# Two-layer decoder on one core: the four value products of the memory attention become one part of TensorE's order, and the orders of four engines are searched anew

## The reference, cut to what matters

```python
x = _layernorm(x + _L0_attn_ref(x, ...))        # station A, windowed
x = _layernorm(x + _L0_xattn_ref(x, ctx, ...))  # station B, cross
x = _layernorm(x + _L0_ffn_ref(x, ...))         # station X, experts
x = _layernorm(x + _L1_attn_ref(x, ...))        # station C, decayed
x = _layernorm(x + _L1_xattn_ref(x, ctx, ...))  # station E, memory
x = _layernorm(x + _L1_ffn_ref(x, ...))         # station F, feed forward
```

## Time and profile before

| | before |
|---|---|
| median of 3 runs | 1128.7 us (1123.98 to 1131.87) |
| profiled execution: its own time | 1128.63 us |
| profiled execution: span of the trace | 1126.8 us |
| PE busy | 989.2 us, 88% of the span |
| DVE busy | 943.9 us, 84% |
| ACT busy | 751.5 us, 67% |
| POOL busy | 145.0 us, 13% |
| mean granted clock of TensorE | 0.959 |

### The profile page before, as it was taken

The page is one execution under the profiler, slowest core; times in us unless marked ns, Lnnn a source line. Parts: engine busy times, 40 slices in busy tenths (PEclk is TensorE's granted clock), DMA queues, the critical chain, the costliest instruction groups (busy, mean ns, idle before and its releaser), DMA issues.

```text
span 1126.8 us, 19792 instructions
## 1 busy us (share of the span) xinstructions
PE 989.2 (88%) x7038; PEld 699.1 (62%) x7038; DVE 943.9 (84%) x2541; ACT 751.5 (67%) x1854; POOL 145.0 (13%) x401
## 2 busy tenths in 40 slices
PE   4877789999999999999999999999999998898642
PEld 2654556676757676767677676757676666565321
DVE  3977666689898989899999989898989896857854
ACT  2233454758686868778686768686877777667653
POOL 2001110101111020202020111111020201010000
PEclk8879999999999999999999999999999999999875
DMA  6922113020211202020303020111202000000000
GB/s 210 332 84 71 31 57 94 1 66 20 66 38 40 64 29 74 20 85 10 94 10 94 1 83 21 57 47 38 65 29 65 11 11 19 1 20 1 10 9 10
DMA packets 36626, 58.90 MB, mean 52 GB/s; under 512 B 6784, under 2 KB 15872, under 8 KB 36016
## 3 DMA queue, kind: packets, MB, share of 16 engines
q1 hardware_dynamic: 36528, 57.64, 16.5%
HBM read 28.65 MB, written 4.19 MB: 29 GB/s over the span
## 4 chain that ended last, share of the span: by engine, by line
DVE 50%; PE 31%; ACT 12%; issue 4%; POOL 2%; DMA 0%; SPq 0%; ACTq 0%; DVEq 0%; POOLq 0%
PE bank_c L443 8%; DVE area_f L1247 8%; PE bank_e L443 6%; PE bank_a L443 5%; DVE area_a L987 5%; DVE neg_top L1180 4%; DVE area_a L1031 4%; ACT squares_out L1321 3%; DVE area_f L1238 3%; PE bank_f L443 3%; DVE x L875 2%; DVE area_f L1256 2%; DVE area_a L1035 2%; PE bank_x L443 2%; DVE area_f L1262 2%
## 5 line engine op out<-in xcount | busy, mean ns | idle before, releaser
L1247 DVE SCALAR_TENSOR_TENSOR area_f<-area_f,w_convw 128x254 f32<-128x254 f32 x256 | 111.9, 479 | 9.2 <-ACT area_f L1542 6.9
L1309 ACT ACTIVATE area_bx<-bank_x 128x512 f32<-128x512 f32 (+1 forms) x144 | 70.1, 498 | 37.9 <-PE bank_x L637 21.5
L1180 DVE TENSOR_REDUCE neg_top<-bank_e 128x4 f32<-128x512 f32 x128 | 80.5, 682 | 11.2 <-PE bank_e L443 10.5
L1542 ACT ACTIVATE area_f<-area_f,w_convb,w_convw 128x256 f32<-128x256 f32 x128 | 70.0, 596 | 27.1 <-DVE area_f L1238 26.8
L987 DVE TENSOR_TENSOR area_a<-area_a 128x512 f32<-128x512 f32 x112 | 73.3, 683 | 11.0 <-ACT area_a L1309 10.0
L1031 DVE TENSOR_TENSOR area_a<-area_a 128x512 f32<-128x512 f32 x112 | 74.5, 684 | 0.9 <-DMA area_a<-area_a 0.6
L1309 ACT ACTIVATE area_a<-bank_a 128x512 f32<-128x512 f32 (+1 forms) x80 | 44.0, 550 | 42.1 <-PE bank_a L443 31.1
L1309 ACT ACTIVATE area_bx<-bank_c 128x512 f32<-128x512 f32 x64 | 34.5, 539 | 53.9 <-PE bank_c L443 51.1
L1513 ACT ACTIVATE area_e<-bank_e 128x512 f32<-128x512 f32 x128 | 68.4, 594 | 1.4 <-PE bank_e L797 1.4
L1035 DVE TENSOR_TENSOR area_a<-area_a 128x512 f32<-128x512 f32 x96 | 65.8, 685 | 0.2
L443 PE MATMUL bank_e<-area_e,chosen_v 128*32 128x512 f32 x256 | 56.9, 604 | 5.1 <-ACT area_e L1513 4.6
(11 more groups left out here) (313 smaller groups left out, 2670.0 us busy)
## 6 DMA issues: line engine op xcount, KB each, us to landing
area_a<-area_a SPq DMA_DIRECT2D x96, 224.0 KB
area_a<-in_xT SPq DMA_DIRECT2D x16, 256.0 KB, 2.9
x<-in_x SPq DMA_DIRECT2D x16, 256.0 KB, 2.9
area_bx<-in_ctxT SPq DMA_DIRECT2D x16, 256.0 KB, 2.6
area_d<-in_ctxT SPq DMA_DIRECT2D x16, 256.0 KB, 2.7
y<-x SPq DMA_DIRECT2D x16, 256.0 KB, 2.2
w_wqkv_e<-in_wqkv_e SPq DMA_DIRECT2D x1, 3072.0 KB, 12.5
area_f<-in_raw SPq DMA_DIRECT2D x2, 1024.0 KB, 11.8
```

The lines of the kernel that those rows point to most:

```text
L1180: dve.tensor_reduce(top[:, b, :, r, 0].rearrange("p (par c) -> p c par", c=DC), bank_e[r][:, :].rearrange("p (c par k) -> p c par k", c=DC ...
L1247: last = dve.scalar_tensor_tensor(c4[:, i, :, dst], h4[:, i, :, src], cwt3[:, 2 * jj + i, k:k + 1], c4[:, i, :, dst], ALU.mult, ALU.add)
L1309: return act.activation(dst, src, ACT.Copy)
L1542: last = act.activation(c4[:, i], h4[:, i], ACT.Identity, bias=w["convb"][:, j:j + 1], scale=cwt3[:, j, 1:2])
```

## The change

On PE the four value products of a sequence become one part: one wait for the fourth exponential, four products, one mark on `e_pv`. Station E has 11 parts a group on PE and no longer 17. ACT's waits on `e_pv` are counted anew: the first exponential of the second sequence waits for the one mark of the first sequence, the other three wait for no product, and the copy to `turned_e` waits for one mark. The arithmetic, the tiles and the DMAs are the same.

The strings of SP, PE, DVE and ACT are others; POOL's is the same. Of what moved, apart from the joined parts:

- PE, groups 1 to 11: the joined products of the second sequence stand where its last three stood before; the single one, which stood between X.10 and C.4 or next to it, is gone. In group 13 the joined products of the second sequence stand behind X15.9, not ahead of it.
- From group 5 on, up to the emptying stage, the orders of PE, DVE and ACT hold only a few short moves; no division (L1197, L1201) changes its place among DVE's large parts.
- Between groups 3 and 4, DVE takes F3.0 ahead of C4.4, and PE takes X6.1 and F3.0 ahead of C4.12 and E4.0 (`FXCACEBFXFAE` becomes `FXCAXFCEB`).
- SP, groups 6 to 15: A.2 is ahead of B.0 of the same turn, not behind it.

```diff
 ORDER = {
     "SP": (
-        "SASABCSASASASSBSSAAABAAABAAACAABACBAACFABAACFABAACFABAACFABAACFABAACFABAACFABAACFABAACFABAACFABACFCFCFFF"
+        "ASSBCASASASSBASSSAAABAAABAAACAAABCBAACFAABACFAABACFAABACFAABACFAABACFAABACFAABACFAABACFAABACFAABCFFCFCFF"
         "F"
     ),
     "PE": (
...
-        "ACAXFCEEEEXCEXCXEXCECFXCEEEXECFECEACACFXCACEBFXFAEBFXABXFBXAEXFBEBAXCAFCEEEEXCEXCXEXCECXFCEEEXECFECEACAX"
...
+        "XCEXECFECEACACFXCAXFCEBFAEBFXABXBFXAEXBFEBAXCFACEXCEXCXEXCCXFCEXECFECEACAXCFCACEBFXFAEBFXABXFBXAEXFBEBAX"
...
     "DVE": (
...
-        "AAAFAFFFECXAFCFEEEEXAEEAFEEAXFAEXFBAFFAAFFBXBFAFFFFXAECFFAAFCACAXAFAAAAEAAAFAFFFECXAFCFEEEEXAEEAFXEEFAAB"
...
+        "AAFAFAFFEXCAFCFEEEEXAEEAFEEAXFAEFXBAFFAAFFBXBFAFFFFXAECFFAAFCACAXAFAAAAEAAAFAFFFEXCAFFCEEEEXAEEFAXEEFAAB"
...
@@ memory(g) on PE
                     yield
+                    pe.wait_ge(e_exp, 8 * g + 4 * b + 4)
                     for r in range(4):
-                        pe.wait_ge(e_exp, 8 * g + 4 * b + r + 1)
-                        mm(bank_e[0][group[r], :], [(mv[:, b, :], pT_e[:, r * 4 * P:(r + 1) * 4 * P])]).then_inc(e_pv, 1)
-                        yield
+                        last = mm(bank_e[0][group[r], :], [(mv[:, b, :], pT_e[:, r * 4 * P:(r + 1) * 4 * P])])
+                    last.then_inc(e_pv, 1)
+                    yield
                     pe.wait_ge(e_pv_out, 2 * g + b + 1)
@@ memory(g) on ACT
                         act.wait_ge(e_logits, 8 * g + 4 * b + r + 1)
-                        if b:
-                            act.wait_ge(e_pv, 8 * g + r + 1)
+                        if b and r == 0:
+                            act.wait_ge(e_pv, 2 * g + 1)
...
-                    act.wait_ge(e_pv, 8 * g + 4 * b + 4)
+                    act.wait_ge(e_pv, 2 * g + b + 1)
                     copy(turned_e, bank_e[0][:, :]).then_inc(e_pv_out, 1)
```

More of the change, by code:

```diff
@@ L79 @@
-        "EEEFEEEEEEEFEFEFFFFFFFFFF"
+        "AAAASAASSBSSBAAASABABAAABBSBXBXAAXAXAXBASXABSXAXABBXXXXXABAXBAXBABXAXAXBXABXCAXCXCXCXXCXCAXCAXCACCACXCAC"
+        "XEBXEBABEBXBEBACXAECXECECXXECXCXCXEAXECECACXACCFCAEBFBEFXABFXBXAEXFBEBACFAXCEXCEXCXEXCCFXCEFXECECEACACFX"
+        "CACXEBFAEFBFXABXFBXAEXFBEBACXAFCEXCEXCXEXCCFXCEXECFECEACACFXCACXEBFAFEBFABXFXBXAEXFBEBACXAFCEXCEXCXEXCCF"
+        "XCEXECFECEACACFXCAXFCEBFAEBFXABXBFXAEXBFEBAXCFACEXCEXCXEXCCXFCEXECFECEACAXCFCACEBFXFAEBFXABXFBXAEXFBEBAX"
@@ new lines @@
+        "CFACEXCEXCXEXCCXFCEXECFECEACAXCFCACXEBFAFEBFXBAXBFXAEXFBEBAXCFACEXCEXCXEXCCXFCEXECFECEACAXCFCACXEBFAFEBF"
+        "XBAFXBXAEXFBEBAXCFACEXCEXCXEXCCXFCEXECFECEACAXCFCACXEBFAFEBFXBAXBFXAEXFBEBAXCFACEXCEXCXEXCCXFCEXECFECEAC"
+        "AXCFCACXEBFAFEBXFBAFXBXAEXFBEBAXCAFCEXCEXCXEXCCXFCEXECFCEAECAXCFCACXEBFAFEBFXBAFXBXAEXFBEBAXCAFCEXCEXCXE"
+        "XCCXFCEXECFECEACAXCFCACXEBFAFEBFBXAFXBXAEXFBEBAXCFACEXCXECXEXCCXFCEXECFECEACAXCFCCXEBFEBFBFXBXFXEXFEBFBX"
+        "CECXECEXCXFXECXCXCXEFECECFCXCCFCEFCFCECFXCEXEFXFXECEXCXEXCFXEXCFXEXECECFCCCECFCEFCFEFCEFECECECFECECCEFEC"
@@ L91 @@
[L91 to L92 removed]
+        "SAAASAAAASSSSAAAAAAAAAAAAAAASASAAAAABAABASABAAAAAAAAAAAAAXAXSXSAAAAASXAABAXABAAAAAXAAAAAAAABXAXAAAXXAABA"
+        "BAXBAXAAAAAAAXAACAAAAACXCAXCXACAAAXAEEEEEEEEEAABBXBAAXEAAAAACXAAAAAACCAAXEEACFCXEEEEAAAAAEEFEXEFEFXBFFAA"
+        "BFFXBFAFFFFXAECFFAAFACCAFXAAAAAAEAFAFAFFEXCAFCFEEEEXEEAAFEEXAFEAFXBAFFAAFFBXBFAFFFFXAECFFAAFACCAXAFAAAAE"
@@ L93 @@
+        "EEEXAEEAFXEEFAAEBAFFAAFXFXBFBFAFFFFXAECFFAAAFCCAXFAAAAAEAAAFAFFXFECAFCFEEEEXAEEAFEEXAFXAEFABFFAABFFXBFFA"
+        "FFFXAEFCAFAFCACXAFAAAAAEAAFAAFFFXECAFCFEEEEXEEEFXEEFBFXFBFFXFFBFFFFXEFFXFCFCCXEFFFFEFCFCXEEEEFFEEEEEFXFC"
+        "FFFFXFFFXFEXFFCCFXFFFFFEXECFCFEEEEEEEEEFFCFFFCFEFCFFFFFFFEFCFEFCFFFEEEEFFEEEEEFFFFFFFFEFFFFFFFEFFFFFEFFF"
         "FFFFFFFFFFFFFFFFFFFF"
@@ L106 @@
-        "FCEFFFXEFFFXEEEFFXCECFXFXEFXCEEEXCCXEFXCFFFEXCXECEFCFCFCFCFEFEEEFECFEFCFFCEEEECCFEFCFFCFECEFCFFFEFFFFFEF"
-        "FFEEEEFFEFFFFEEEFEFEEFFFFEEFFFFFFFFFFFFFFFFFFFFFF"
+        "AASASSASASBSSBAAAASABABABABBBXBXAAAAXAXBAXXABABXXXXXSABXBBXAXBAAXBAAXBXBXAXBCAXBCXCXXCXCXCAXXCCACXACACAA"
+        "CXBXBBEBXBEEEEABCXAEBCXCEEEEXCXCXEXCCXCEACXXECEAXCAAFCABFBFABXFFXBFEFXBFFEEEEACFXFACBFEXCFXBXCEFCEXEECXE"
+        "CCCEFCFFFAEXECAXFXCAFAXBFAFBFABXFXFBEFFXBFEEFEEACXFAFCBEFXCFXBXCEFCEXEECXECCCEFCFFFAEXECAXFXCAFAXBFAFBFA"
@@ new lines @@
+        "BXFFXBFEXFBFEFEEEACXFAFCBEFXCFXXBCEFCEXEECXECCCECFFFFAEXECAXFXAFCAFXBFABFABXFXBFEFXFBFEEFEEACXFAFCBEFXCB"
+        "XFXCEXCFEEEXCECCCECFFFAFEXECAXFXCAFABFXFABFABXFXFFBEXFBFFEEEECAXFFACEBFXCFXBXCEFCXEEECXECCCECFFFAFXECAXE"
+        "XFCAAFXBFAFBFBAXFXFBEFXFBFFEEEEACXFFCBAEFXCFXBXCECXFEEECXECCCECFFFAFXECAXEXFCAAFXBFFABFBAXFXFBEFFXBFFEEE"
+        "ACXEFFCABEFXCFXBXCEXCFEEEXCECCCECFFFAFXECAXEXFCAAFXBFFABFBAXFXFBEFXFBFFEEEAECXFAFCEBFXCFXBXCEXCFEEECXECC"
+        "CECFFFAFEXCAEXXFCAAFXBFFABFABXFXFBEFXFBFFEEEAECXFAFCBEFXCFXBXCEFCXEEEXCECCCCEAFFFFXEXACXEFACAFXBFFABFBAX"
@@ L108 @@
+        "FXBFEFXFBFEEFEAXCFEAFCBEFXCFXBXCEFCXEEECXECCCECFFFAFEXCAEXXFCAAFXBFFABFBAXFXFBEFXFBFFEEEEAXCFFACBFEXBCXF"
+        "XCEFCXEEEXCECCCEFCFFAFXECAXEXACFXFBFBFBFXFXBFEFXFFEBEFEEXFCFEBCFXFBCFEXEXEECXECXCXCCEFCFFFXCEXEFCXFCFFCF"
+        "CFCEFFXEFFXFEEFEFXCECFXFXEFXCEEEXCCEXCFXFFFEXCXECEFCFCFCFCFEFEEEFECFFECFFCEEEECCFEFCFFCFECEFCFFFEFFFFFEF"
+        "FFEEEFEFFEFFEEEEFFEFEFFFFEEFFFFFFFFFFFFFFFFFFFFFF"
     ),
```

32 lines of the change are left out of this document (4 added, 28 removed).

## The result

The changed kernel takes 1132.44 us (median of 22 runs, 1130.25 to 1136.73) against 1130.28 us (22 runs) of the kernel before beside it: a ratio of 1.0026, 95% interval 1.0017 to 1.0036. A second comparison on another chip gave 1.0041 (1.0024 to 1.0058). So it is slower, by 2 to 5 us. The forecast was 1127.4 us, with no difference that can be measured as the likeliest; 1132.4 lies in the range (1116 to 1134) and within 1% of the kernel before, but the kernel moved the other way than forecast. A profiled execution of the changed kernel took 1134.5 us, with a span of 1132.7 us.

A forecast was written before the change was run, and what follows sets the result against it. The prediction took DVE's long piece and PE's short piece of each even-stage turn as the bound. Terms -1.96 - 0.54 + 1.25 = -1.25 us against 1128.63 us gave 1127.4 us, range 1116 to 1134.

The forecast's parts named there:

- What bounds the kernel: Even stage: DVE's work in the long piece or PE's in the short one sets the turn, despite PE's 96% busy.
- The half case: Rival: groups 1 to 11 gain some 0.5 us each as PE's lead helps ACT and DVE; 1121 us, chance 0.14.
- the case of PE as the bound: Rival: all 14 freed value product slots count, 13.7 us; 1116.2 us, chance 0.11.
- the late keys: Groups 3 to 4, keys' copy behind DVE's scaling: +1.25 us net, at most +1.74; as slower rival 1130.4 to 1133.4, chance 0.09.
- The split: An even-stage turn loops through two pieces: DVE fills 591.9 to 641.4 us, PE fills 581.3 to 591.9 us.
- the short piece: Part of a turn from 581.3 to 591.9 us, from the transposes of `att_e`; PE busy 10.56 of 10.60 us.
- The slots on the path: Single value products on the chain, groups 9 and 13: 0.98 us saved each; group 11: DVE's wait of 0.54 us goes.
- The other moves: Reordered parts, mostly in the filling and emptying stages: bounded at 3 us either way, taken as 0.
- The wait for the fourth exponential: Joined products wait for nothing in group 6 and end at the same time in group 15's emptying stage: cost 0.
- The clock rival: Rival: PE's longer wait before the even stage's transposes drops its clock; up to 95 us more, 1222 us, chance 0.03.

The follow-up runs named there:

- joined_alone: Kernel before, its order kept, with the four value products joined behind one wait for the fourth exponential: 1130.41 us, ratio 0.9998.
- spend_slot: Changed kernel, groups 1 to 11: memory attention's second division one station A product sooner on DVE, weights' copy directly behind the exponential on ACT: 1138.92 us, ratio 1.0069.
- turn4_full: Changed kernel with the turn from group 3 to 4 back in the order of before on every engine: 1131.35 us, ratio 1.0022.
- joined_four: Kernel before, its order kept, with the four value products joined, each waiting for its own exponential: 1126.56 us, ratio 0.9969; again 1126.51 us, 0.9973.
- fill_joint: best_fill with the joint wait for the fourth exponential everywhere: 1129.08 us, ratio 0.9998 to the kernel before.
- tail_four: Kernel before, value products joined: joint wait in groups 0 to 13, separate waits for each exponential in groups 14 and 15: 1127.39 us, ratio 0.9990.
- turn4_old: Changed kernel with the turn from group 3 to 4 only partly in the order of before, ACT's copy of chosen values staying late: 1134.55 us, ratio 1.0034.
- best_fill: joined_four plus products of ones into a free bank ahead of PE's waits in group 15: 1123.20 us, ratio 0.9925; again 1123.31 us, 0.9949.

## Why the prediction was wrong

**What bounds the kernel: right in what it was used for.** The claim that PE's 96% doesn't make it the bound held: joined_alone does 10 us less on PE in the even stage and takes the same time. The half case and the case of PE as the bound are out. (The half case's 1121 us also left out the late keys' 1.25 us.) The split was too clean: spend_slot shows that DVE reaches into the short piece by way of ACT.

**The slots on the path: half right.** Group 13's 0.98 us is there (54.5 to 53.6 us in joined_alone), but the new order's turn is 54.2 to 54.4, so the changed kernel keeps 0.2 to 0.3 of it. Group 9's slot gave nothing, and group 11's 0.2 to 0.3 us of 0.54. The step "I take the whole slot" fails for groups 9 and 11: with the single product gone, the next product waits 0.83 us for ACT's copy. Both bounds (0 and the slot) were given; the wrong one was taken. That joining with separate waits gains some 3 us in all, near the 2.5 forecast, is in part luck, since the places named give about 1.2 of it; where the rest comes from stays open.

**The late keys: right.** Forecast +1.25 us, at most +1.74; the turn grew by 1.5 us, DVE waits 2.23 us, and turn4_full gives the 1.5 us back in its trace. Its 2.25 us in the medians agree, but aren't clear of the noise.

**The other moves: within the bound, taken as 0.** The new order costs 3 to 5 us in the table of four cells, 1.5 of them by the late keys. Of the rest, 0.6 us from group 11 to 12 and the 0.7 that the new order takes from group 13's slot can be placed. What is left is near or within the 3 us; its middle, 0, had nothing behind it.

**The wait for the fourth exponential: the step that failed.** The prediction set the end of the last exponential beside the end of the last pass, found one pass between them, and wrote "Joined, they end at the same time. Cost 0." That holds at the upper clock: the last product starts 4.21 us behind the logits either way. What it left out is that the three early products also kept PE at work through the wait. Without them PE is idle for 3 us, and the passes behind run at the lower level, 2.24 us in one sequence of group 14. The clock rival was there at 0.03, with the right mechanism in the wrong stage: it was looked for at the transposes of the even stage, where waits stay short, and priced at 95 us. In the emptying stage, where the earlier trace rows already showed 0.86 and the earlier trace rows a wait of 1.59 us, it was not looked for. The term put at 0 measures 3 to 5 us in the table of four cells. Of that the traces place 1.06 and 2.24 us in the first sequence of group 14, in two executions; that the clock is the cause is shown there, and only likely for the rest, in group 15.

**Sum.** Beside the forecast of -1.25: late keys +1.5, group 12 +0.6, the other turns -0.8 to -1.1, last two turns +3.2 (second profile) to +6.0, filling stage -1.1 to -2.1, behind the last group 0 to +1.1. That makes +3.5 and +5.9 us for the two profiles; the medians differ by 2.2 and 5.1. The last two turns are the part that one profile settles least, since the clock's falls differ between executions of one kernel.

**What stays open.** Why the fillers gave 3.2 to 3.4 us in joined_four, some 3 to 4 in the changed kernel, and nothing in the kernel before and, against joined_alone, in fill_joint (0.9998 both). Why the first `wc1x` product comes anywhere between 218.4 and 224.7 us. Why the clock falls behind the same waits in one execution and not in the next. And whether the joint wait costs anything ahead of group 14 (tail_four against joined_four).

## What to carry to other kernels

Joining small steps for one wait takes work off a waiting engine, and that work can be what keeps its clock up: before costing such a wait at nothing, look at what TensorE does during it and at the granted clock of that stretch, above all in the emptying stage. An instruction on the chain is worth its length only down to the next wait behind it, here 0.15 of 0.98 us. When two parts of a change each seem to cost nothing, fill in the fourth cell of the table: here both halves cost 3 us, hidden by what joining gained. And where TensorE must wait in the last groups, cheap products into a free bank can pay, but it has to be measured: joined products with separate waits and such fillers took 1123.2 us, 0.5 to 0.75% less than the kernel before, on two chips, while in the kernel before itself they gave nothing.

## What the hardware showed unexpectedly

The even stage, at 1.00 in every other profile, fell to 0.50 for 3 us in turn4_old, behind a single stretch of 2 us in which PE was busy for 0.20 us, and the scores behind it took 2.09 us where 1.15 is usual. Behind the same waits of 0.85 and 0.31 us in the emptying stage the same product took 2.09 us in one execution and 1.15 in another. A kernel with 13 us more of PE work than its twin (985.9 against 972.5 us busy, best_fill against joined_four) was 3.4 us quicker.
